# Two kinds of subtraction move from VectorE to GpSimd: the low parts of split weights, and the last step of rounding the feed-forward weights

## What is computed

```python
x = x + attention(layernorm(x))             # 16 heads of 32, causal
x = x + cross(layernorm(x), ctx_512)        # 32 query heads of 16 on 8 key heads, no weights
x = x + mx_ffn(layernorm(x))                # gate, up, down
x = x + state_space(layernorm(x))           # scan over 256 steps, 32 heads x 128 states
x = x + causal_cross(layernorm(x), ctx_512)
x = x + lora_experts(layernorm(x))          # dense product, top 2 of 8 experts of rank 16
```

```python
amax  = max(|x|) over the block;  scale = 2 ** (floor(log2(amax)) - 2)
y     = x / scale
step  = 2 ** (max(floor(log2(|y|)), 0) - 1)
q     = clip(round(y / step) * step, -6, 6) * scale
```

## Time and profile before

| | us |
|---|---|
| three runs: median (lowest to highest) | 1620.25 (1616.87 to 1622.1) |
| profiled execution, its span from first to last instruction | 1615.7 |
| TensorE busy, share of the span | 1374.8, 85% |
| VectorE busy | 1347.9, 83% |
| ScalarE busy | 1038.7, 64% |
| GpSimd busy | 423.9, 26% |

### The profile page before, as it was taken

The page is one execution under the profiler, slowest core; times in us unless marked ns, Lnnn a source line. Parts: engine busy times, 40 slices in busy tenths (PEclk is TensorE's granted clock), DMA queues, the critical chain, the costliest instruction groups (busy, mean ns, idle before and its releaser), DMA issues.

```text
span 1615.7 us, 31163 instructions
## 1 busy us (share of the span) xinstructions
PE 1374.8 (85%) x12080; PEld 729.4 (45%) x12080; DVE 1347.9 (83%) x2015; ACT 1038.7 (64%) x1884; POOL 423.9 (26%) x488
## 2 busy tenths in 40 slices
PE   3778888879899999889978777879999999999986
PEld 2443445334445453444443333436455555555542
DVE  6989989979879888887898899978698888978743
ACT  3244365465673865756585768985799788989430
POOL 1432041132341522322331240241222313122210
PEclk9687979799999999999999988889999999999987
DMA  6313112200201111002130003111020211101020
GB/s 227 93 53 93 52 49 66 74 14 1 74 14 40 36 40 41 21 22 54 51 100 28 1 1 138 27 27 44 2 70 2 69 34 38 40 5 44 4 77 26
DMA packets 54194, 76.38 MB, mean 47 GB/s; under 512 B 8353, under 2 KB 23713, under 8 KB 53537
## 3 DMA queue, kind: packets, MB, share of 16 engines
q1 hardware_dynamic: 54048, 74.40, 16.3%
HBM read 39.24 MB, written 9.44 MB: 30 GB/s over the span
## 4 chain that ended last, share of the span: by engine, by line
PE 48%; DVE 29%; ACT 10%; issue 7%; POOL 3%; DMA 1%; SPq 0%; ACTq 0%; DVEq 0%; POOLq 0%
PE bank L193 17%; DVE mix_NM L1058 4%; PE bank L1158 4%; PE bank L526 3%; PE bank L534 2%; PE bank L514 2%; DVE ssm_HS L1518 2%; PE bank L971 2%; DVE ffn_m L1112 2%; PE bank L487 2%; DVE ffn_Z L1122 2%; PE bank L549 2%; PE bank L931 2%; PE bank L956 2%; DVE ffn_room L1130 1%
## 5 line engine op out<-in xcount | busy, mean ns | idle before, releaser
L1031 ACT ACTIVATE mix_P<-bank 128x512 f32<-128x512 f32 x256 | 142.2, 603 | 52.6 <-PE bank L956 50.7
L1058 DVE TENSOR_REDUCE mix_NM<-bank 128x2 f32<-128x512 f32 x256 | 164.4, 683 | 10.5 <-PE bank L931 9.8
L714 POOL TENSOR_SCALAR_AFFINE_SELECT cross_P<-cross_P 128x256 f32<-128x256 f32 x128 | 87.9, 696 | 280.3 <-ACT cross_P L628 280.0
L1276 POOL TENSOR_TENSOR ffn_room<-ffn_room 128x512 f32<-128x512 f32 x64 | 90.9, 1421 | 266.9 <-ACT ffn_room L1215 170.0
L1518 DVE TENSOR_TENSOR_SCAN ssm_HS<-ssm_DA,ssm_DD 128x1024 f32<-128x1024 f32 x64 | 150.2, 2347 | 11.4 <-ACT ssm_DD L1469 6.6
L714 POOL TENSOR_SCALAR_AFFINE_SELECT attn_P<-attn_P 128x256 f32<-128x256 f32 x128 | 86.3, 686 | 247.0 <-ACT attn_P L628 246.9
L1466 ACT ACTIVATE ssm_DA<-ssm_Z,A_T 128x255 f32<-128x255 f32 x256 | 110.8, 498 | 2.4 <-DVE ssm_HS L1518 2.1
L628 ACT ACTIVATE attn_P<-bank 128x384 f32<-128x384 f32 x128 | 63.8, 498 | 64.7 <-PE bank L515 64.2
L628 ACT ACTIVATE cross_P<-bank 128x384 f32<-128x384 f32 x128 | 62.7, 490 | 52.3 <-PE bank L515 51.7
L1524 DVE TENSOR_TENSOR ssm_HS<-ssm_HS,ssm_CS 128x1024 f32<-128x1024 f32 x64 | 80.7, 1261 | 0.9
L1441 ACT ACTIVATE ssm_Z<-bank 128x512 f32<-128x512 f32 x128 | 72.2, 598 | 13.6 <-PE bank L1354 12.9
(11 more groups left out here) (408 smaller groups left out, 4072.9 us busy)
## 6 DMA issues: line engine op xcount, KB each, us to landing
attn_stack<-attn_P SPq DMA_DIRECT2D x96, 128.0 KB, 2.4
cross_stack<-cross_P SPq DMA_DIRECT2D x96, 128.0 KB, 2.5
ffn_room<-f_gate SPq DMA_DIRECT2D x4, 1024.0 KB, 5.9
XR<-x SPq DMA_DIRECT2D x8, 512.0 KB, 6.4
ffn_room<-f_up SPq DMA_DIRECT2D x4, 1024.0 KB, 5.5
ffn_room<-f_down SPq DMA_DIRECT2D x4, 1024.0 KB, 5.5
x_mid<-XR SPq DMA_DIRECT2D x8, 512.0 KB, 3.0
XR<-x_mid SPq DMA_DIRECT2D x8, 512.0 KB, 3.8
```

The costliest lines, as they stand in the source:

```text
L714: nc.gpsimd.affine_select(out=diagonal, in_=diagonal, compare_op=ALU.is_ge, fill=0.0, base=0, pattern=[[0, 2], [1, P]], channel_multiplier ...
L1031: nc.scalar.activation(self.p[h % 8], bank[b4[h % 2]][:, :], ACT.Exp, scale=HD2 ** -0.5).then_inc(s["p_ready"], 1)
L1058: nc.vector.tensor_reduce(self.nm[:, t, 16 * i + 2 * g:16 * i + 2 * g + 2], bank[b4[u % 3]][:, :].rearrange("p (c k) -> p c k", c=2), AX.X ...
L1276: nc.gpsimd.tensor_tensor(self.inter[q % 2][:, 512 * (g % 2):512 * (g % 2) + 512], self.sg[g % 2], self.up[g % 2], ALU.mult).then_inc(s["i ...
```

## The change

Two subtractions go to GpSimd, and the turns of all engines are written anew.

```diff
             # class Loader
-            def dve(self, dve, i):
+            def pool(self, pool, i):
                 yield
                 w = self.items[i][0]
-                dve.wait_ge(self.high_ready, self.first + i + 1)
-                nc.vector.tensor_tensor(w.low, self.staged(i), w.high, ALU.subtract).then_inc(self.low_ready, 1)
+                pool.wait_ge(self.high_ready, self.first + i + 1)
+                nc.gpsimd.tensor_tensor(w.low, self.staged(i), w.high, ALU.subtract).then_inc(self.low_ready, 1)
...
             # class Quantised
-            def dve(self, dve, own, i):
+            def dve_scale(self, dve, own, i):
...
-                scaled = own(nc.vector.tensor_scalar(q_sc, q_e, 0.25, None, ALU.mult))
+                own(nc.vector.tensor_scalar(q_sc, q_e, 0.25, None, ALU.mult))
                 yield
                 own.wait(mark)
-                mark = own(nc.vector.tensor_tensor(blocks(y), blocks(y), broadcast(q_inv, 2, BLOCK), ALU.mult))
...
+                self.scaled = own(nc.vector.tensor_tensor(blocks(y), blocks(y), broadcast(q_inv, 2, BLOCK), ALU.mult))
+
+            def dve_align(self, dve, own, i):
+                y, c = self.raw[i % 2], self.c
+                yield
+                own.wait(self.scaled)
+                if i:
+                    dve.wait_ge(self.rounded, i)
                 mark = own(nc.vector.tensor_scalar(c.bitcast(I32), y.bitcast(I32), EXPONENT, None, ALU.bitwise_and))
...
-                mark = own(nc.vector.scalar_tensor_tensor(y, y, 6.0, c, ALU.min, ALU.add))
-                yield
-                own.wait(mark)
-                mark = own(nc.vector.tensor_tensor(y, y, c, ALU.subtract))
...
+                nc.vector.scalar_tensor_tensor(y, y, 6.0, c, ALU.min, ALU.add).then_inc(self.aligned, 1)
+
+            def dve_finish(self, dve, i):
+                blocks = lambda t_: t_.rearrange("p (n b) -> p n b", b=BLOCK)
+                yield
+                dve.wait_ge(self.rounded, i + 1)
                 if i:
                     dve.wait_ge(self.w_ps, 2 * i)
...
+            def dve(self, dve, own, i):
+                if i < len(self.units):
+                    yield from self.dve_scale(dve, own, i)
+                if i:
+                    yield from self.dve_finish(dve, i - 1)
+                if i < len(self.units):
+                    yield from self.dve_align(dve, own, i)
+
+            def pool(self, pool, i):
+                y = self.raw[i % 2]
+                yield
+                pool.wait_ge(self.aligned, i + 1)
+                nc.gpsimd.tensor_tensor(y, y, self.c, ALU.subtract).then_inc(self.rounded, 1)
```

More of the change, by code:

```diff
@@ L31 @@
[L31 to L40, removed]
@@ L745, in __init__ @@
                 self.w16 = room[:, 6144:7168].bitcast(BF16)
-                self.q_max, self.q_e, self.q_inv, self.q_sc = (
-                    sb(st, f"w_{part}", [P, 2048 // BLOCK])[:, :] for part in ("max", "e", "inv", "sc"))
+                self.q_max, self.q_e, self.q_inv, *self.q_sc = (
+                    sb(st, f"w_{part}", [P, 2048 // BLOCK])[:, :] for part in ("max", "e", "inv", "sc0", "sc1"))
                 self.raw_in = [sem(f"w_raw_in{i}") for i in range(2)]
-                self.w16_ready, self.w_ps, self.w_ready = (sem(f"w_{part}") for part in ("w16", "ps", "ready"))
+                self.w16_ready, self.w_ps, self.w_ready, self.aligned, self.rounded = (
+                    sem(f"w_{part}") for part in ("w16", "ps", "ready", "aligned", "rounded"))
                 self.units = []
@@ L1940, in _ @@
                              in_turn(lambda n: ffn.dve(dve, own, n)),
-                             in_turn(lambda i: quantised.dve(dve, own, i), units),
+                             in_turn(lambda i: quantised.dve(dve, own, i), units + 1),
                              in_turn(lambda n: ssm.norm.dve(dve, own, row1, loaded_middle, n)),
@@ L1948, in _ @@
                              in_turn(lambda n: lora.norm.dve(dve, own, row1, crossed, n)),
-                             in_turn(lambda n: lora.dve(dve, own, n)),
-                             in_turn(lambda i: weights_0.dve(dve, i), items_0),
-                             in_turn(lambda i: weights_a.dve(dve, i), items_a),
-                             in_turn(lambda i: weights_f.dve(dve, i), items_f))
+                             in_turn(lambda n: lora.dve(dve, own, n)))
                 own.wait()
@@ L1972, in _ @@
                              in_turn(lambda n: cross.pool(pool, B + n)),
-                             in_turn(lambda n: lora.norm.pool(pool, own, n)))
+                             in_turn(lambda n: lora.norm.pool(pool, own, n)),
+                             in_turn(lambda i: weights_0.pool(pool, i), items_0),
+                             in_turn(lambda i: weights_a.pool(pool, i), items_a),
+                             in_turn(lambda i: weights_f.pool(pool, i), items_f),
+                             in_turn(lambda i: quantised.pool(pool, i), units))
         clear(numbers)
```

118 lines of the change are left out of this document (63 added, 55 removed).

## The result

The changed kernel takes 1699.67 us (median of 4, 1693.53 to 1710.92), the kernel before 1620.01 (median of 4 beside it). The ratio is 1.0492, 95% interval [1.0446, 1.0538]: 80 us slower, where 1612 was forecast and 1638 was the upper end. The profiled execution spans 1708.6 us, against 1615.7. It is the slowest of the four runs, 11 us above their median, so what is read from it at its end (93 us behind) is more than the 80 us.

A forecast was written before the change was run, and what follows sets the result against it. VectorE was taken as the limit from 55 to 366 us. Start 20 late, 4 of 15 standing still, 2 for masks, 41 less work: -8, so 1612 us; 8-in-10 range 1590 to 1638.

The forecast's parts named there:

- the last sentence of the sum: After 366 us: all engines' work as before, beginning earlier by what was gained; profiled span 1615.7 would become 1607.7 us.
- a late start: Up to the first score maximum: 10 to 28 us later than before, 20 taken in the sum.
- given back to TensorE: Rival, chance 0.19: the first stretch's gain is lost after 366 us, TensorE 88% busy and masks late; 1617 to 1624 us.
- the start and GpSimd's queue: Rival, chance 0.32: start 28 us late, six subtractions late by 2 us each behind masks in GpSimd's in-order queue; 1634 us.
- The credit: After the first score maximum, up to the feed-forward part: VectorE has 37.5 + 3 = 41 us less to do.
- The mechanism of the earlier trace: VectorE steps with two SBUF tensors, or fast single-tensor ones, stand still for a whole GpSimd instruction reading SBUF; maxima do not.
- the term of 15.4 us: Units from the fourth on: VectorE standing still under GpSimd's subtraction, 15.4 us in all, 4 of it taken in the sum.
- First score maximum: At the start: first score maximum, line 665, at 65 to 83 us, 10 to 28 later than before.
- Line 648: At the start, behind line 822: 39.6 us if nothing blocked, 43 to 58 us with GpSimd's steps in the way.
- the 25 us taken: At the start: 31 us from products' start to first maximum before, less 6.0 of waiting for low parts, leaves 25.
- Line 822 4.52 us, forecast 4.7: GpSimd's subtraction of 2048 values: 4.7 us, twice its 2.35 us for a sum of 1024; same for a big low part.
- Low parts of the second layer: Second layer: 16.5 us less on VectorE against 7 low parts, 33 us on GpSimd, half of it blocking; net zero.

The follow-up runs named there:

- late_new_turns: The kernel before, nothing moved to GpSimd, with every engine's turns from 366 us on taken from the new order: 1674.7 us, ratio 1.0331.
- after_then_old: The changed kernel with both moves and its own turns up to 376 us, and the old turns behind it: 1657.8 us, ratio 1.0229 to the kernel before.
- early_new_turns: New turns and two-deep units up to 376 us, old turns after, low parts and subtraction on VectorE: 1646.8 us, 1.0156 to the kernel before.
- The experiment on the 27.8 us: The kernel before with the twelve subtractions left out altogether and the sum ahead of them made a minimum: 1612.7 us, ratio 0.9942.
- new_none: The changed kernel's turns and two-deep units, with low parts and subtraction back on VectorE: 1696.5 us, ratio 1.0471 to the kernel before.
- new_sub: The changed kernel with only the low parts back on VectorE, the subtraction staying on GpSimd: 1699.8 us, ratio 1.0495 to the kernel before.
- old_sub: The kernel before, old turns, only each unit's last subtraction on GpSimd, the next unit's maximum pulled ahead as cover: 1640.0 us, ratio 1.0120.

## Why the prediction was wrong

**The step that failed** is the last sentence of the sum: "After 366 us all engines' work is as before and begins earlier by what was gained." But for the low parts, which the prediction itself had put at zero, the work is as before; the order is not. New turns from there on cost 54 us with nothing moved (late_new_turns), and 42 us with the moves made (after_then_old). I read the new strings only where the prediction's terms rested on them, and gave an order no price of its own. The 25 us of the first stretch (early_new_turns) are another matter: for a late start the sum had 20.

This is about half of the miss of 88 us. The other half was there by 366 us: the sum had the changed kernel 8 us ahead at that point, and its lag was 34 behind. Of those 42 us the start is 8, and the credit, next, is the larger part: 29 at the rate given there, an estimate.

The rival "given back to TensorE" had the place (behind 366 us), but was priced at 5 to 12 us above the forecast and rested on late masks, not on the order. The rival that ended on the slower side, the start and GpSimd's queue, had the sign, but not the cause: the queue made line 806 wait once in the changed kernel, 6.7 us.

**The credit.** "It has 37.5 + 3 = 41 us less to do" was taken in full. The experiment on the 27.8 us of it gives 7 to 9 us. VectorE at 278 of 311 us was the busiest engine, but with time taken off it the same turns wait for TensorE and ScalarE instead: a quarter to a third of it reaches the end. With 41 us credited at that rate, some 12, the sum would have been about +20 instead of -8. In the changed kernel the credit never showed: the lag was 28 us at the first score maximum and 34 at 350 us. Up to its last line 806 VectorE was idle for 72 of 371 us; before, up to the same step, for 47 of 362. What it waited for up to 372 us (waiting instruction, releaser, us in all, times, longest):

```profile
DVE mix_RS L1092 <- PE bank L1006: 15.5, 3, 8.5
DVE w_max L772 <- DMA ffn_room<-f_gate: 12.9, 2, 12.0
DVE mix_P L1072 <- ACT mix_P L1028: 9.5, 2, 9.1
DVE w_max L772 <- DMA ffn_room<-f_up: 5.0, 2, 4.6
```

In the kernel before the same four were 6.8, 0, 0.6 and 0. (The wait of 12.0 is the program's begin, where VectorE before waited 13.7 us for ScalarE; so the loads of raw weights are 5.9 us more, for which the sum had no term.)

**Standing still.** The mechanism of the earlier trace rows is right, and was shown again at the small steps. The ten groups of lines that both kernels run for the units take 196.8 us after and 158.0 before, 38.8 more (189.1 and 155.6, 33.5 more, where records that overlap are counted once). This is not the term of 15.4 us, which was for the fourth unit on. There the size was about right. Line 775 from the fourth unit on, and line 774 before:

```profile
L775 DVE TENSOR_SCALAR w_max<-w_max 128x64 f32<-128x64 f32 x9 | 13.6, 1512 | 0.1
L774 DVE TENSOR_SCALAR w_max<-w_max 128x64 f32<-128x64 f32 x9 | 1.8, 201 | 0.2
```

That is 11.8 us more, and the three small steps behind it are as short as before (6.1 us in both). So one lock for each unit, as I had charged, is what the trace shows there. The rest fell in the first three units: their small steps took 33 us instead of 4, since GpSimd had several instructions queued without a gap (lines 284, 708, 891, 394 and 396 besides 822), and then each dependent step met one of its own. The Trainium skill's rule (SBUF — State Buffer, "Who interferes with whom") names both kinds, two-input steps and fast single-input ones, and holds here. In time all this was again worth little in the new order, where new_none, free of it, is 3 us faster. Debit and credit were in the same coin, VectorE's busy time, and neither was the time of the kernel.

**The start.** First score maximum 65 to 83 us, 20 later taken: it came at 83.7, 28 later, against 55.6 in the earlier trace rows, 0.7 us over the range. Line 648, forecast at 43 to 58, came at 53.1, with GpSimd's steps slipping in between as I had named for the upper end. The rest of the way was longer than the 25 us taken: 28 from the products' start at 55.6. In it the third unit's small steps held VectorE from 59.9 to 69.6 us, beside line 822 and the two clearings of `attn_stack`, which my working does not mention. new_none has the first maximum at 68.6: 13 us are the new order, with the units and Wq and Wk ahead of x, and 15 the moves. With the low parts alone on the old turns it is 61.7.

**Durations.** Line 822 4.52 us, forecast 4.7: right. (The 4.5 us of the Trainium skill's GPSIMD Engine Reference, "Elementwise — side-by-side cycle accounting", was the better figure; this trace agrees with it.) Line 284 on 2048 values 4.05 us, forecast 4.7: too long by 0.65. Low parts of the second layer: "zero", and 7 of them; they are twelve, and took GpSimd 35 us against the 33 taken. On the old turns the low parts' lag grew from 10 to 14 and to 19 us at their two places there, so some 9 us in that profile, not zero; in the new order they cost nothing that can be told (new_sub).

**What stays open.** Which of the displaced turns cost the 54 us isn't settled, nor which engine's string: the place at 549 us is an example, and the lag grows in both layers. Exchanging one engine's string alone wasn't tried.

## What to carry over

Where every engine follows a written order, the order is a term of its own, and here it was the largest: before pricing what a change moves, compare the order in all stretches that it does not mean to touch, and ask of each engine what it will now stand in front of. Time an engine gives up is worth only what removing the work altogether gives, so measure that first (here a quarter to a third). A long two-tensor instruction on GpSimd can cost VectorE its length for each short step that meets it; a chain of short dependent steps meets one of them if GpSimd's queue has one, and one for each step if it has many in a row.

## What the runs showed of the hardware

- GpSimd: 128 x 2048 f32 minus f32 in 4.50 to 4.55 us; f32 minus f16 into f16 in 4.05, 512 columns in 1.15 (each is what most records show; beside VectorE single ones are longer, up to 4.87 in old_sub and 6.04 in the changed kernel). Cutting the first into four gained nothing (1644.0 against 1640.0 us).
- A VectorE step of 0.2 us lasted up to 4.02 us beside such an instruction, and one of 2.3 us 6.19. GpSimd's clearing of 32 x 4096 does the same to a fast single-tensor step: the first row is VectorE's, the second GpSimd's.

```profile
62.47 3.53 DVE L777 TENSOR_SCALAR w_e<-w_max 128x64 int32<-128x64 int32 x1
```

```profile
62.44 3.51 POOL L394 MEMSET attn_stack<- 32x4096 f16 x1
```

- An order disturbed at random by 0.7 of a place on average, on two engines, costs 26% of the time here. Part of it comes through TensorE's granted clock: 0.97 to 0.88 behind 366 us, with TensorE busy for 1159 us instead of 1058.
